# Key attention: partial sums of the probabilities on GpSimd, the rest on VectorE

## The chip, the cores and the metric

The kernel runs on one core of one Trainium2 chip. A core has TensorE (PE in the profile, its weight loads PEld), VectorE (DVE), ScalarE (ACT), GpSimd (POOL) and SyncE (SP, which issues DMAs here). Each engine takes its own instructions in order; engines wait for one another by semaphores. The metric is the device time of one execution in microseconds.

## The reference, cut to what matters

The whole reference is four layers of cross attention and feed-forward on an input x of 64 x 64 x 128. The change is in the feed-forward of the first layer, which is an attention with 16 heads of 8 channels, in which the softmax runs over the queries of each key. Its sum is taken over the 64 queries of a sequence:

```python
z = layernorm(x)
q, k, v = split_heads(z @ Wq), split_heads(z @ Wk), split_heads(z @ Wv)
scores = einsum('bkd,bqd->bkq', k, q) / sqrt(128)
attn = softmax(scores, axis=-1)
out = einsum('bkq,bkv->bqv', attn, v)
```

After it come the output projection, two normalizations and a gelu.

## The kernel before, in words

The work is cut into 32 tiles of two sequences, 128 rows each. `key_attention0_stage` (L592) treats one tile after another in a software pipeline. For each engine, `pipeline` (L58) is given a list of steps with a lag: in round t the engine issues, in the order of the list, step f for tile t - lag. With `straight=True` all rounds are written out, 32 rounds and as many more as the longest lag. Nothing is reordered at run time: an instruction whose semaphore is not there yet holds up everything behind it on its engine. `done(eng, sem, u)` waits until the semaphore's event for tile u has come, and `free(eng, sem, u, bufs)` waits for tile u - bufs, so that a buffer can be taken again.

For one tile the steps are these, with the names that the profile shows behind the stage's prefix f_:

- VectorE takes the statistics of the layer norm (`vector_stats`, L231, lag 0) and makes mean and variance of them (`vector_moments`, L241, lag 1).
- GpSimd turns the variance into 1 / sqrt(variance + eps) in two small instructions (`pool_rstd`, L247 and L250, lag 1). This is its only work in the rounds.
- VectorE applies mean and factor (`vector_apply`, L257, lag 2) and TensorE transposes the result and projects it.
- TensorE makes the scores of 16 heads in two halves (L753). VectorE takes the maximum over the 64 queries (L650) and subtracts it (L654), for each half (lag 5), and writes into `Pr`, a ring of six tiles of 128 x 16 x 64.
- ScalarE takes the exponential in place (L705), TensorE multiplies later with the probabilities that are not yet divided.
- VectorE, in `divide_v` (lag 7), sums the 64 probabilities of each head (L661), takes the reciprocal (L664) and multiplies the values by it (L668).
- TensorE multiplies values and probabilities (L767) and makes the output and the next layer's keys and values (L779 to L785); ScalarE squares and copies them (L715 to L720).

The order within a round is that of the lists. VectorE's is apply, softmax of half 0, softmax of half 1, moments, stats, divide_v (L676). GpSimd's list has the one step (L639). The next stage begins when all engines have ended this one.

Of the kernel before, what the change touches and what calls it, by code (L numbers as in the profile page):

```python
# [16 lines left out]
ALU = mybir.AluOpType  # L17
ACT = mybir.ActivationFunctionType
AX = mybir.AxisListType.X

P = 128
B, T, D = 64, 64, 128
NT = B // 2
# [34 lines left out]
def pipeline(eng, n, steps, straight=False, period=2):  # L58

    lags = [lag for lag, _ in steps]
    head = -(-(max(lags) + period) // period) * period
    if straight or head >= n:
        head = n

    def static(t):
        for lag, fn in steps:
            if 0 <= t - lag < n:
                fn(t - lag, (t - lag) % period)  # L70

    for t in range(head):
        static(t)
    if head < n:
        with eng.Fori(head // period, n // period) as i:
            for p in range(period):
                for lag, fn in steps:
                    fn(period * i + (p - lag), (p - lag) % period)
    for t in range(n, n + max(lags)):
        static(t)  # L80


def done(eng, sem, u, per=1):

    eng.wait_ge(sem, per * u + per)


def free(eng, sem, u, bufs=2, per=1):

    if isinstance(u, int) and u < bufs:  # L90
        return
    eng.wait_ge(sem, per * u + (per - per * bufs))
# [39 lines left out]
HEADS = 16  # L132
# [3 lines left out]
class Net:  # L136
# [6 lines left out]
    def w(self, name, lo=0, hi=None):  # L143
        at, n = COLS[name]
        return self.W[:, at + lo:at + (n if hi is None else hi)]


def opener(net, ctx, stage):


    nc = net.nc
    net.stale, net.current = net.current, []

    def sb(name, shape, dt=F32):
        return ctx.enter_context(nc.sbuf_tensor(f"{stage}_{name}", shape, dt))

    def ps(name, shape, dt=F32):
        return ctx.enter_context(nc.psum_tensor(f"{stage}_{name}", shape, dt))

    def sem(name):  # L160
        net.current.append(ctx.enter_context(nc.semaphore(f"{stage}_{name}")))
        return net.current[-1]

    return sb, ps, sem
# [427 lines left out]
def key_attention0_stage(net):  # L592
    nc, X, w = net.nc, net.X, net.w
    SCALE = D ** -0.5
    SG, HG, RING, DEPTH = 4, 4, 8, 6
    with ExitStack() as ctx:
        sb, ps, sem = opener(net, ctx, "f0")
# [4 lines left out]
        Pr = sb("Pr", [P, DEPTH, HEADS, T])  # L602
        mx = sb("mx", [P, 2, HEADS])
        sums = sb("sums", [P, 2, HEADS])
# [12 lines left out]
        s_spread = sem("spread")  # L617
        s_S, s_mx, s_sub, s_exp, s_sum = sem("scores"), sem("max"), sem("sub"), sem("exp"), sem("sum")
        s_rd, s_vs, s_z, s_zt, s_y = sem("rden"), sem("v_out"), sem("z"), sem("zt"), sem("y")
        s_sq, s_wz, s_wzs = sem("squares"), sem("wowff"), sem("wowff_out")  # L620
        s_cX = [sem("cX_even"), sem("cX_odd")]
        ln = LayerNorm(net, sb, sem, xn, s_xt)
        block = ctx.enter_context(nc.Block())

        @block.sync
        def _(sp):
            clear_stale(net, sp)

            def load_context(u, p):
                free(sp, s_y, u)  # L630
                sp.dma_start(cX[:, p, :], net.dram["ctxT"][u]).then_inc(s_cX[p], 16)
            pipeline(sp, NT, [(0, load_context)], straight=True)

        @block.gpsimd
        def _(pool):
            ln.setup(pool)
            nc.gpsimd.memset(V[:], 0.0).then_inc(s_zero, 1)

            pipeline(pool, NT, [(1, lambda u, p: ln.pool_rstd(pool, u, p))],  # L639
                     straight=True)  # L640

        @block.vector
        def _(dve):
            def softmax(half):
                def fn(u, p):
                    Sg = S[:, half, :, 0:256].rearrange("p r (h k) -> p r h k", k=T)
                    top = mx[:, p].rearrange("p (r u h) -> p r u h", r=2, u=2)[:, :, half]
                    out = Pr[:, u % DEPTH].rearrange("p (r u h) k -> p r u h k", r=2, u=2)[:, :, half]
                    dve.wait_ge(s_S, 2 * u + half + 1)
                    nc.vector.tensor_reduce(top, Sg, AX, ALU.max).then_inc(s_mx, 1)  # L650
                    dve.wait_ge(s_mx, 2 * u + half + 1)
                    free(dve, s_z, u, bufs=DEPTH)
                    free(dve, s_sum, u, bufs=DEPTH)
                    nc.vector.tensor_tensor(out, Sg, top.unsqueeze(3).broadcast_to([P, 2, HG, T]),  # L654
                                            ALU.subtract).then_inc(s_sub, 1)
                return fn

            def divide_v(u, p):
                done(dve, s_exp, u)
                free(dve, s_rd, u)  # L660
                nc.vector.tensor_reduce(sums[:, p, :], Pr[:, u % DEPTH], AX, ALU.add).then_inc(s_sum, 1)  # L661
                done(dve, s_sum, u)
                free(dve, s_vs, u)
                nc.vector.reciprocal(rden[:, p, :, 0], sums[:, p, :]).then_inc(s_rd, 1)  # L664
                done(dve, s_rd, u)
                free(dve, s_z, u)
                dst = V[:, p].rearrange("p g (h c) -> p g h c", c=40)[:, :, :, 0:8]
                nc.vector.tensor_tensor(dst, qkv[:, u % RING, 2].rearrange("p (g h c) -> p g h c", g=SG, h=HG),  # L668
                                        rden[:, p].rearrange("p (g h) c -> p g h c", g=SG).broadcast_to([P, SG, HG, 8]),
                                        ALU.mult).then_inc(s_vs, 1)  # L670

            dve.wait_ge(s_zero, 1)
            dve.wait_ge(s_wz, 1)
            nc.vector.tensor_copy(wow[:, D:2 * D], pA[:, 0:D]).then_inc(s_wzs, 1)
            nc.vector.tensor_copy(wow[:, 0:D], w("f0_wo")).then_inc(s_wzs, 1)
            pipeline(dve, NT, [(2, lambda u, p: ln.vector_apply(dve, u, p)), (5, softmax(0)), (5, softmax(1)),  # L676
                               (1, lambda u, p: ln.vector_moments(dve, u, p)),
                               (0, lambda u, p: ln.vector_stats(dve, u, p)), (7, divide_v)], straight=True)

        @block.scalar  # L680
# [1959 lines left out]
def feed_forward0(net):  # L2640
    key_attention0_stage(net)
# [153 lines left out]
```

## Time and profile before

| | |
|---|---|
| median of three runs | 1559.8 us (1554.31 to 1561.81) |
| the profiled execution | 1556.68 us |
| its span, first to last instruction | 1554.9 us |
| TensorE busy | 1308.1 us, 84% of the span |
| VectorE busy | 1018.9 us, 66% |
| ScalarE busy | 861.1 us, 55% |
| GpSimd busy | 599.4 us, 39% |
| mean granted clock of TensorE | 0.914 |

The shares are means over five stages with different limits. The stage of the change runs from about 243 to 422 us. Between the profiled execution's time and its span lie 1.8 us that the trace does not show.

### The profile page before, as it was taken

The page shows a single profiled execution, that of the slowest core. Times are in us where ns is not written, and L with a number is a line of the kernel's source. Part 1 is how long each engine was busy: PE and PEld are TensorE (multiplying, and loading weights), DVE is VectorE, ACT ScalarE, POOL GpSimd, SP SyncE. Part 2 cuts the span into 40 slices and gives each one's busy share as a digit, 9 for nine tenths or more (in the row PEclk, how much of TensorE's full clock was granted, in tenths as well). Part 3 has the DMA queues.
Part 4 walks back from the last instruction along what each step waited for, and adds up shares of the span by engine and source line. Part 5 has one row for each costly group of instructions (what it writes and reads, how often), then busy time and mean ns, then how long its engine had stood idle before and what let it go on. Part 6 is the DMA issues. An engine that isn't in the chain of part 4 may idle for free. (4 is left out here: it accounts for less than half of the span.)

```text
span 1554.9 us, 43292 instructions
## 1 busy us (share of the span) xinstructions
PE 1308.1 (84%) x15204; PEld 1006.5 (65%) x15204; DVE 1018.9 (66%) x3181; ACT 861.1 (55%) x2287; POOL 599.4 (39%) x1092
## 2 busy tenths in 40 slices
PE   5999997999679999768999599899549975777797
PEld 3677764555446666658999467677449964666576
DVE  4788855999698887533444477775612114888886
ACT  2666653777678697652222145455224435777686
POOL 4555521111065476460000375574530017663232
PEclk9999996999989999799999789999769995888899
DMA  3423220000100000156776311122113321111001
GB/s 116 174 104 116 109 92 5 13 17 17 38 2 1 2 22 21 37 176 189 207 206 204 93 44 53 59 88 68 62 56 115 105 72 43 35 37 31 12 14 42
DMA packets 101759, 112.52 MB, mean 72 GB/s; under 512 B 11456, under 2 KB 83136, under 8 KB 101440
## 3 DMA queue, kind: packets, MB, share of 16 engines
q1 hardware_dynamic: 73792, 83.75, 17.1%
q0 software_dynamic: 8192, 16.79, 3.8%
q10 hardware_dynamic: 19584, 9.44, 2.1%
q8 instruction: 118, 1.93, 0.5%
q14 instruction: 73, 0.60, 0.1%
HBM read 69.05 MB, written 40.89 MB: 71 GB/s over the span
## 5 line engine op out<-in xcount | busy, mean ns | idle before, releaser
L2404 ACT ACTIVATE a_silu<-a_banks 128x256 f32<-128x256 f32 x120 | 42.4, 382 | 126.9 <-DVE a_y L2279 89.7
L2567 PE MATMUL a_banks<-a_rowsT,a_w_up 128*128 128x256 f32 x480 | 111.8, 383 | 0.0
L489 ACT ACTIVATE a_PT<-a_ST 128x1024 f32<-128x1024 f32 x64 | 65.5, 1024 | 76.1 <-PE a_ST L556 76.1
L444 DVE TENSOR_REDUCE a_mx<-a_S 128x8 f32<-128x1024 f32 x64 | 78.1, 1220 | 32.2 <-PE a_S L529 32.0
L2567 PEld LDWEIGHTS a_banks<-a_rowsT,a_w_up 128*128 128x128 f32 x480 | 89.3, 193 | 10.8
L1154 ACT ACTIVATE a_h<-a_SO,a_w_down 128x256 f32<-128x256 f32 x128 | 50.2, 474 | 65.3 <-PE a_SO L1319 65.3
L2272 DVE TENSOR_TENSOR a_h<-a_silu,a_banks 128x256 f32<-128x256 f32 x120 | 47.5, 419 | 58.0 <-ACT a_silu L2404 57.9
L218 POOL MEMSET a_ln_half<- 128x1 f32 x3 | 0.3, 100 | 220.5 <-POOLq L1900 183.6
L1070 DVE COPY a_rowsT<-a_pX 128x256 f32<-128x256 f32 x32 | 13.6, 424 | 108.1 <-PE a_pX L1308 108.1
L529 PE MATMUL a_S<-a_qkM,a_qk 32*128 32x512 f32 x256 | 78.3, 689 | 6.1 <-DVE a_mx L444 6.1
L1095 ACT ACTIVATE a_xT<-a_pQ 128x128 f32<-128x128 f32 (+1 forms) x44 | 14.3, 325 | 117.3 <-PE a_pQ L1184 84.2
L923 POOL DMA_INDIRECT slots_in<-R,r_put x64 | 63.1, 985 | 36.6 <-DVE r_put L1040 19.5
L548 PE MATMUL a_ST<-a_qkM,a_qk 32*128 32x512 f32 x256 | 72.6, 643 | 1.4 <-ACT a_PT L489 1.4
L2600 POOL DMA_INDIRECT R<-slots_out,r_get x64 | 62.5, 977 | 19.5 <-issue 19.5
L2600 POOL DMA_INDIRECT Y<-slots_out,r_get x64 | 64.0, 1001 | 14.2 <-issue 13.9
L2453 PE MATMUL a_banks<-a_spread,a_blk 128*128 128x512 f32 x128 | 67.6, 610 | 0.0
L1330 PEld LDWEIGHTS a_pT<-a_w_down,a_h 128*128 128x128 f32 x512 | 62.1, 192 | 2.4 <-issue 0.8
L1330 PE MATMUL a_pT<-a_w_down,a_h 128*128 128x128 f32 x512 | 62.4, 275 | 0.6 <-DVE a_y L1079 0.6
L1319 PE MATMUL a_SO<-a_rowsT,a_w_up 128*128 128x256 f32 x256 | 62.7, 389 | 0.0
L2577 PEld LDWEIGHTS a_banks<-a_w_down,a_h 128*128 128x128 f32 x480 | 59.8, 192 | 2.8 <-issue 0.8
L2577 PE MATMUL a_banks<-a_w_down,a_h 128*128 128x128 f32 x480 | 60.1, 275 | 0.6 <-DVE a_y L2279 0.6
L480 ACT ACTIVATE a_qkM<-a_qk,W 128x256 f32<-128x256 f32 x128 | 54.2, 496 | 8.0 <-POOL a_qk L387 7.9
(423 smaller groups left out, 4105.1 us busy)
## 6 DMA issues: line engine op xcount, KB each, us to landing
slots_in<-Y SPq DMA_DIRECT2D x32, 512.0 KB, 3.3
a_w_up<-in_f_dram SPq DMA_DIRECT2D x40, 384.0 KB, 3.1
a_rows<-slots_in SPq DMA_DIRECT2D x72, 128.0 KB, 2.6
slots_out<-a_y ACTq DMA_DIRECT2D x72, 128.0 KB, 2.6
a_w_down<-in_f_dram SPq DMA_DIRECT2D x40, 192.0 KB, 2.9
keys_ahead<-a_ahead SPq DMA_DIRECT2D x8, 512.0 KB, 3.4
a_k<-keys_ahead SPq DMA_DIRECT2D x8, 512.0 KB
W<-in_wpack_dram SPq DMA_DIRECT2D x1, 3276.5 KB, 11.9
```

The source lines that it names most:

```text
L444: nc.vector.tensor_reduce(mx[:, p % 2, 2 * half:2 * half + 2], S[:, :, :].rearrange("p g (h k) -> p g h k", k=D), AX, ALU.max).then_inc(s_ ...
L480: i = nc.scalar.activation(qkM[:, p, :, j, :], qk[:, p], ACT.Copy, scale=w("mask4")[:, j:j + 1])
L489: nc.scalar.activation(PT[:, p % 2, 2 * half:2 * half + 2].rearrange("p g h k -> p g (h k)"), ST[:, :, :], ACT.Exp, scale=SCALE).then_inc( ...
L529: i = nc.tensor.matmul(S[:, b, :], qk[r, p, 0, :], qkM[r, p, 1].rearrange("p h k -> p (h k)"), start=True, stop=True)
L548: nc.tensor.matmul(ST[:, b, :], qk[r, p, 1, :], qkM[r, p, 0].rearrange("p h k -> p (h k)"), start=True, stop=False)
L923: nc.gpsimd.indirect_dma_start(xg[:, :], bass.IndirectOffsetOnAxis(ap=rt.put[:, kk, v:v + 1], axis=0), R[:, v, :], None).then_inc(s_put, 16)
L1319: i = nc.tensor.matmul(H[:, BANKS * p + b, CHUNK * c:CHUNK * (c + 1)], up[:, e % 2, lo:lo + P], rowsT[:, p, :], start=True, stop=True)
L1330: i = nc.tensor.matmul(pY[:, D * s:D * s + D], h[:, p, c, P * s:P * s + P], down[:, e % 2, D * c:D * (c + 1)], start=(c == 0), stop=(c == ...
L2453: nc.tensor.matmul(S[:, g, :], blk[:, p, g, :], spread[:, p, g].rearrange("p h t -> p (h t)"), start=False, stop=True).then_inc(s_S, 1)
L2567: i = nc.tensor.matmul(H[:, HC * p + b, CHUNK * c:CHUNK * (c + 1)], up[:, p, at:at + P], rowsT[:, p, :], start=True, stop=True)
L2577: i = nc.tensor.matmul(pE[:, D * s:D * s + D], h[:, p, c, P * s:P * s + P], down[:, p, D * c:D * (c + 1)], start=(c == 0), stop=(c == HC - 1))
L2600: net.nc.gpsimd.indirect_dma_start(t[:, u, :], None, rows, bass.IndirectOffsetOnAxis(ap=rt.get[:, k, u:u + 1], axis=0)).then_inc(rt.s_got[ ...
```

## The change

GpSimd gets a second step, `fold`, with lag 7. For each tile it adds the right 32 of the 64 probabilities of each head to the left 32 (`halves`), waits for its own result, and adds the right 16 of these to the left 16 (`quarters`). VectorE's sum in `divide_v` then runs over these 16 numbers of each head instead of over 64, and waits for `quarters` instead of for the exponential. The subtraction that writes into `Pr` again waits for `halves` in place of the sum. Both new tiles have two buffers.

```diff
--- before.py
+++ after.py
@@ -617,6 +617,8 @@
         s_spread = sem("spread")
         s_S, s_mx, s_sub, s_exp, s_sum = sem("scores"), sem("max"), sem("sub"), sem("exp"), sem("sum")
         s_rd, s_vs, s_z, s_zt, s_y = sem("rden"), sem("v_out"), sem("z"), sem("zt"), sem("y")
+        s_half, s_quarter = sem("halves"), sem("quarters")
+        halves, quarters = sb("halves", [P, 2, HEADS, T // 2]), sb("quarters", [P, 2, HEADS, T // 4])
         s_sq, s_wz, s_wzs = sem("squares"), sem("wowff"), sem("wowff_out")
         s_cX = [sem("cX_even"), sem("cX_odd")]
         ln = LayerNorm(net, sb, sem, xn, s_xt)
@@ -636,7 +638,17 @@
             ln.setup(pool)
             nc.gpsimd.memset(V[:], 0.0).then_inc(s_zero, 1)
 
-            pipeline(pool, NT, [(1, lambda u, p: ln.pool_rstd(pool, u, p))],
+            def fold(u, p):
+                done(pool, s_exp, u)
+                free(pool, s_quarter, u)
+                nc.gpsimd.tensor_tensor(halves[:, p], Pr[:, u % DEPTH, :, 0:T // 2], Pr[:, u % DEPTH, :, T // 2:],
+                                        ALU.add).then_inc(s_half, 1)
+                done(pool, s_half, u)
+                free(pool, s_sum, u)
+                nc.gpsimd.tensor_tensor(quarters[:, p], halves[:, p, :, 0:T // 4], halves[:, p, :, T // 4:],
+                                        ALU.add).then_inc(s_quarter, 1)
+
+            pipeline(pool, NT, [(1, lambda u, p: ln.pool_rstd(pool, u, p)), (7, fold)],
                      straight=True)
 
         @block.vector
@@ -650,15 +662,15 @@
                     nc.vector.tensor_reduce(top, Sg, AX, ALU.max).then_inc(s_mx, 1)
                     dve.wait_ge(s_mx, 2 * u + half + 1)
                     free(dve, s_z, u, bufs=DEPTH)
-                    free(dve, s_sum, u, bufs=DEPTH)
+                    free(dve, s_half, u, bufs=DEPTH)
                     nc.vector.tensor_tensor(out, Sg, top.unsqueeze(3).broadcast_to([P, 2, HG, T]),
                                             ALU.subtract).then_inc(s_sub, 1)
                 return fn
 
             def divide_v(u, p):
-                done(dve, s_exp, u)
+                done(dve, s_quarter, u)
                 free(dve, s_rd, u)
-                nc.vector.tensor_reduce(sums[:, p, :], Pr[:, u % DEPTH], AX, ALU.add).then_inc(s_sum, 1)
+                nc.vector.tensor_reduce(sums[:, p, :], quarters[:, p], AX, ALU.add).then_inc(s_sum, 1)
                 done(dve, s_sum, u)
                 free(dve, s_vs, u)
                 nc.vector.reciprocal(rden[:, p, :, 0], sums[:, p, :]).then_inc(s_rd, 1)
```

## Rows read from the trace of the kernel before

**Rows 1.** windows, full pipeline: busy us (instructions), granted clock, DMA share, GB/s

```profile
266.70:389.20 122.50, 112.71 (x2515) 71.45 (x2512) 119.03 (x251) 94.44 (x331) 18.45 (x50) 0.95 0.05 15
```

**Rows 2.** timeline of VectorE over one round: start us, us, engine, line, operation

```profile
291.19 0.17 DVE L241 BATCH_NORM_AGGREGATE f_ln_moments<-f_ln_stats 128x2 f32<-128x6 f32 x1
...
291.45 1.20 DVE L661 TENSOR_REDUCE f_sums<-f_Pr 128x16 f32<-128x1024 f32 x1
292.69 0.25 DVE L664 RECIPROCAL f_rden<-f_sums 128x16 f32<-128x16 f32 x1
...
293.18 0.34 DVE L257 TENSOR_SCALAR f_xn<-X,f_ln_moments,f_ln_rstd 128x128 f32<-128x128 f32 x1
...
296.09 0.17 DVE L241 BATCH_NORM_AGGREGATE f_ln_moments<-f_ln_stats 128x2 f32<-128x6 f32 x1
```

**Rows 3.** timeline of GpSimd, same round; brackets: idle us before, releaser

```profile
291.44 0.19 POOL L247 TENSOR_TENSOR f_ln_rstd<-f_ln_moments,f_ln_half 128x1 f32<-128x1 f32 x1 [4.08 <-DVE f_ln_moments L241]
...
291.70 0.55 POOL L250 TENSOR_TENSOR f_ln_rstd<-f_ln_rstd,f_ln_half 128x1 f32<-128x1 f32 x1
```

**Rows 4.** VectorE's instructions grouped by shape: count, busy us, mean ns, idle before

```profile
L2219 DVE TENSOR_REDUCE a_dense<-a_t 128x32 f32<-128x256 f32 x2 | 0.8, 420 | 0.1
```

**Rows 5.** timeline in the stage before this one, GpSimd and VectorE

```profile
141.45 0.55 POOL L250 TENSOR_TENSOR a_ln_rstd<-a_ln_rstd,a_ln_half 128x1 f32<-128x1 f32 x1
...
141.97 0.73 POOL L383 TENSOR_TENSOR a_rot<-a_rot 128x256 f32<-128x256 f32 x1
...
142.87 0.82 DVE L257 TENSOR_SCALAR a_xn<-X,a_ln_moments,a_ln_rstd 128x128 f32<-128x128 f32 x1
142.87 0.73 POOL L387 TENSOR_TENSOR a_qk<-a_rot,a_qbias 128x256 f32<-128x256 f32 x1 [0.17 <-POOL a_rot L383]
```

**Rows 6.** GpSimd's instructions grouped by shape, the whole execution

```profile
L2062 POOL TENSOR_TENSOR a_spread<-a_biased,W 128x512 f32<-128x512 f32 x32 | 33.4, 1042 | 5.5 <-PE a_banks L2453 3.4
...
L387 POOL TENSOR_TENSOR a_qk<-a_rot,a_qbias 128x256 f32<-128x256 f32 x32 | 23.6, 738 | 3.9 <-POOL a_rot L383 2.7
...
L2067 POOL TENSOR_TENSOR X<-X,W 128x128 f32<-128x128 f32 x32 | 15.5, 483 | 0.0
```

**Rows 7.** timeline where VectorE waits for GpSimd's second rstd instruction

```profile
244.13 0.55 POOL L250 TENSOR_TENSOR f_ln_rstd<-f_ln_rstd,f_ln_half 128x1 f32<-128x1 f32 x1
244.79 0.34 DVE L257 TENSOR_SCALAR f_xn<-X,f_ln_moments,f_ln_rstd 128x128 f32<-128x128 f32 x1 [0.83 <-POOL f_ln_rstd L250]
```

**Rows 8.** timeline of the stage's last rounds, VectorE and then ScalarE

```profile
389.22 0.17 DVE L241 BATCH_NORM_AGGREGATE f_ln_moments<-f_ln_stats 128x2 f32<-128x6 f32 x1
...
390.53 0.25 DVE L664 RECIPROCAL f_rden<-f_sums 128x16 f32<-128x16 f32 x1
...
406.49 0.69 DVE L654 TENSOR_TENSOR f_Pr<-f_S,f_mx 128x512 f32<-128x512 f32 x1
...
410.68 0.28 ACT L715 ACTIVATE f_junk<-f_pY 128x128 f32<-128x128 f32 x1 [1.29 <-PE f_pY L785]
...
420.79 0.28 ACT L715 ACTIVATE f_junk<-f_pY 128x128 f32<-128x128 f32 x1 [1.47 <-PE f_pY L785]
```

**Rows 9.** windows of two other stretches, columns as in the first group

```profile
1000.00:1010.00 10.00, 6.80 (x107) 5.30 (x105) 6.72 (x26) 3.24 (x7) 8.12 (x11) 1.00 0.17 50
1470.00:1480.00 10.00, 6.05 (x18) 3.39 (x17) 6.68 (x31) 5.38 (x14) 3.81 (x8) 0.50 0.02 4
```

**Rows 10.** timeline of TensorE, granted clock 0.50 until about 277 us

```profile
271.55 0.80 PE L738 MATMUL f_pA<-f_xT,W 128*128 128x128 f32 x2
...
276.77 0.80 PE L738 MATMUL f_pA<-f_xT,W 128*128 128x128 f32 x2
...
281.75 0.45 PE L779 MATMUL f_pY<-f_cX,W 128*64 128x64 f32 x8
...
283.00 0.66 PE L753 MATMUL f_S<-f_spread,f_qkv 32*64 32x256 f32 x8
```

## Prediction

> **What bounds the kernel now.** The diff touches one stage, the key attention (243 to 422 us), so I read the windows of that stage first, then one round of its pipeline instruction by instruction. From 266.7 to 389.2 us the pipeline is full: VectorE is busy 119.03 of 122.50 us, TensorE 112.71, ScalarE 94.44, GpSimd 18.45 [rows 1]. VectorE is the bound. The timeline of one round shows why: from one aggregate of layer-norm statistics to the next it takes 296.09 - 291.19 = 4.90 us, without idle time, and 1.20 us of it is the sum over the probabilities [rows 2]. GpSimd does two tiny instructions in a round and then waits 4.08 us, each time for VectorE's aggregate [rows 3]. This last column is the one to read: GpSimd is idle, but its work in a round begins only when VectorE has given it the moments.
>
> **The change, part by part.** Call round t the t-th pass over VectorE's list: apply(t-2), the two halves of softmax(t-5), moments(t-1), stats(t), divide_v(t-7). GpSimd's round t becomes rstd(t-1), then fold(t-7). Both are written straight, in order.
>
> *Removed from VectorE.* The sum goes from 1024 elements into 16 to 256 into 16. The nearest row is a reduction of 256 elements into 32, 0.42 us [rows 4]. So it saves 1.20 - 0.42 = 0.78 us a round [rows 2, 4].
>
> *Added to GpSimd.* An add of 128x512 and one of 128x256. For the second there are rows of the same size, 0.73 us (mean 738 ns) [rows 5, 6]. For the first the nearest row is L2062, 128x512 in 1.04 us, but both its operands are broadcasts; L2067 (128x128) takes 0.48 us in the mean and L387 (128x256) 0.74 [rows 6]. A straight line through these two gives 0.74 + 2 x 0.255 = 1.25 us; twice the 128x256 row gives 1.48. I take 1.28, between the line and the row with full operands doubled, nearer to the line, and keep 1.04 and 1.48 as bounds. Between the two adds lies a wait on GpSimd's own semaphore: L387, which waits in the same way for L383, shows 0.17 us of idle time [rows 5]; its lower bound I set at 0.08, the gap between the aggregate's end (291.19 + 0.17) and GpSimd's start at 291.44 [rows 2, 3].
>
> The Trainium skill (GPSIMD Engine Reference, section 3.1) speaks against such a move: it gives 4497 ns on GpSimd against 2293 ns on VectorE for an fp32 add of 2048 elements, because two inputs share one read port. By an estimate pro rata from that page the two adds would be 1.12 and 0.56 us, 0.33 less than my 2.01, and the sum below 8.6 us less. The trace agrees on the direction; its 128x256 row is dearer than pro rata, so the rows are used.
>
> *The wait that is added.* divide_v(t-7) now waits for fold(t-7). The data are old: the exponential of a tile runs right after its second subtraction, two rounds before its sum. But fold(t-7) stands behind rstd(t-1) in GpSimd's queue, and rstd(t-1) waits for moments(t-1), which VectorE issues in the same round t, two instructions ahead of divide_v(t-7). So the fold cannot begin before the moments of the same round, and VectorE stands still until it is finished. Behind the waiting sum on VectorE stand the reciprocal, the product for V, the next apply and the next softmax; TensorE and ScalarE wait for these.
>
> The chain, from the start of the aggregate (291.19 is 0):
> - first rstd instruction at +0.25, second at +0.51 [rows 2, 3]
> - next GpSimd instruction 0.52 after the second (141.45 to 141.97) [rows 5]: halves at +1.03
> - halves 1.28 and the wait 0.17: quarters at +2.48; quarters 0.73: done at +3.21
> - GpSimd's end to VectorE's start, 244.13 + 0.55 to 244.79, 0.11 [rows 7]: sum at +3.32
> - sum 0.42 and 0.04 to the next instruction (as 291.45 + 1.20 to 292.69) [rows 2]: reciprocal at +3.78.
>
> Before, the reciprocal starts at 292.69, +1.50 [rows 2]. So a round is 2.28 us longer: 7.18 in place of 4.90 us. The statistics (about 0.2 us) lie under the chain in either case.
>
> *How many rounds.* A round has this chain where it holds both a moments and a divide_v: t = 7 to 32, 26 rounds. The last of them has no statistics; its reciprocal stands at 390.53 - 389.22 = 1.31 before [rows 8], so it loses 2.47. Together 25 x 2.28 + 2.47 = 59.5 us. In rounds 33 to 38 there is no rstd, GpSimd runs ahead, and the shorter sum is pure gain. Three of these sums (tiles 26 to 28) precede the last subtraction at 406.49; after it ScalarE and TensorE set the end, draining the last outputs at 2.53 us each (410.68 to 420.79, four steps) [rows 8]. So 3 x 0.78 = 2.3 us come back. ScalarE, 3.78 us a round when full [rows 1] and less where no new tiles come in, leaves room for it. The later sums gain nothing.
>
> *Rest.* The subtraction waits for halves instead of sums of six tiles before, long done; two more semaphores are cleared and two small buffers taken: nothing, since SP and memory wait for no one there (if that cover were gone, a few tenths of a us once).
>
> Sum against the profiled execution: 1556.7 + 59.5 - 2.3 = 1613.9 us. That execution lies 3.1 us under the median of the three runs shown, 1559.8, which would give 1617.0. I say **1615**.
>
> Bounds of the costs: with 1.04 us and 0.08 us of wait a round loses 1.95, and the sum is 26 x 1.95 - 2.3 = +48, 1605; with 1.48 us and a quarters add 0.1 us dearer it loses 2.58, +65, 1622.
>
> **The rivals.**
> *The fold is hidden and the change gains.* Place: GpSimd's queue. If fold(t-7) were served before rstd(t-1), VectorE would find it done. For it: GpSimd is idle 4.08 us a round, and the fold needs about 2.2 [rows 3, 5, 6]. Price: 0.78 us less in each of 26 + 3 rounds, -23 us, 1534. It would gain less where the two engines get into each other's way: the apply at L257 takes 0.34 us alone and 0.82 us when it starts together with GpSimd's add at 142.87 [rows 2, 5], which here would take back 0.48 of the 0.78, 1548. It decides as soon as quarters end less than 0.26 us after the aggregate starts, where the sum stands now [rows 2]. Against it: GpSimd's list is in order, and the row of its idle time names the aggregate. 4 in 100.
>
> *TensorE becomes the bound at the lower clock.* The stage is at 0.95 of the full clock before [rows 1]. TensorE's 112.71 us in 25 rounds are 4.51 a round, 92% of 4.90 and 63% of 7.18. Other stretches at about that share show both levels: 6.80 of 10 us busy at a granted clock of 1.00 (2.4 GHz), 6.05 of 10 at 0.50 (1.2 GHz) [rows 9]. At the lower level one round of TensorE without the output projection is 271.55 to 276.77, 5.22 us without a gap; the projection is 283.00 - 281.75 = 1.25 at the full clock, and I bound it at 2.0 to 2.5 at half [rows 10]. That is 7.2 to 7.7 us a round against VectorE's 7.18: 0 to 0.5 us more in each of 26 rounds, up to +13, and a few us in the drain, which hangs on TensorE too. 1617 to 1632, say 1627. Against it: in the stage before, the clock rose to full in the round in which TensorE had no gap left (after 276.77 the same instructions are shorter), and a TensorE that becomes the bound has no gap. 13 in 100.
>
> *The adds are dearer than any row.* The new operands are 16 pieces of 32 and of 16 elements in a row, and the rows here have long pieces [rows 6]. Half as much again on both, 1.0 us a round, gives 1640. 5 in 100.
>
> **How the numbers follow.** The forecast with its bounds 1605 to 1622 has 78 in 100. The range reaches down to 1601, the lower bound less the scatter of the runs (7.5 us from lowest to highest, half of it), and up to 1630, which takes in most of the case of the clock. It leaves out the gain, the dearest adds and a tail. A measurement of this kernel can tell about 0.5%, 8 us, from no change. Faster by more than that: 0.04; within it: 0.01, if the fold were hidden and the gain eaten; slower: 0.95, all other cases.
>
> **What would show it.** Right: in the full rounds VectorE is idle some 2.8 us just before the sum, released by GpSimd's quarters; rounds are 7.2 us apart; halves start 0.52 us after the second rstd instruction; the sum takes 0.42 us; in the last six rounds that idle time is gone. Wrong: halves that start before the aggregate of their round, a halves add outside 1.0 to 1.5 us, TensorE at 1.2 GHz through the stage with scores waited for by VectorE's maximum, or a stage that is not 45 to 75 us longer.

## The result, and the profile after

The changed kernel takes 1614.37 us (median of three runs, 1612.24 to 1615.17) against 1559.8: 54.6 us more. The ratio is 1.033, with an interval of 1.028 to 1.038. Its profiled execution took 1615.17 us, with a span of 1613.3. One of the eight runs of the last experiment below took 3042.9 us, about twice the others, and its ratio leaves that run out.

VectorE's timeline over one full round, from aggregate to aggregate; it answers to [rows 2]:

```profile
288.19 0.17 DVE L241 BATCH_NORM_AGGREGATE f_ln_moments<-f_ln_stats 128x2 f32<-128x6 f32 x1
288.27 0.26 DVE L231 BATCH_NORM_STATS2 f_ln_stats<-X 128x6 f32<-128x128 f32 x1
291.33 0.42 DVE L673 TENSOR_REDUCE f_sums<-f_quarters 128x16 f32<-128x256 f32 x1 [2.79 <-POOL f_quarters L648]
291.78 0.25 DVE L676 RECIPROCAL f_rden<-f_sums 128x16 f32<-128x16 f32 x1
...
295.19 0.17 DVE L241 BATCH_NORM_AGGREGATE f_ln_moments<-f_ln_stats 128x2 f32<-128x6 f32 x1
```

The round is 295.19 - 288.19 = 7.00 us long. The sum is down from 1.20 to 0.42 us, but ahead of it VectorE now stands idle for 2.79 us, released by the quarters. GpSimd's timeline in the same round shows what it waits for, beside [rows 3]:

```profile
288.44 0.19 POOL L247 TENSOR_TENSOR f_ln_rstd<-f_ln_moments,f_ln_half 128x1 f32<-128x1 f32 x1 [4.14 <-DVE f_ln_moments L241]
288.71 0.55 POOL L250 TENSOR_TENSOR f_ln_rstd<-f_ln_rstd,f_ln_half 128x1 f32<-128x1 f32 x1
289.22 1.26 POOL L644 TENSOR_TENSOR f_halves<-f_Pr 128x512 f32<-128x512 f32 x1
290.56 0.74 POOL L648 TENSOR_TENSOR f_quarters<-f_halves 128x256 f32<-128x256 f32 x1
```

GpSimd still waits for the aggregate, here 4.14 us, and starts the halves 0.51 us after the second instruction of the factor. All four instructions lie between the aggregate and the sum. The waits of the stage, 267 to 445 us (us in total, times, longest), show the two engines waiting for each other by turns:

```profile
POOL f_ln_rstd L247 <- DVE f_ln_moments L241: 107.2, 26, 4.1
DVE f_sums L673 <- POOL f_quarters L648: 69.9, 25, 2.8
```

The second line is the only wait of VectorE that the profile lists in that stretch; there is none for TensorE.

GpSimd's groups by shape give the price of the two adds, beside [rows 6]:

```profile
L644 POOL TENSOR_TENSOR f_halves<-f_Pr 128x512 f32<-128x512 f32 x32 | 40.5, 1264 | 8.0 <-ACT f_Pr L717 8.0
...
L648 POOL TENSOR_TENSOR f_quarters<-f_halves 128x256 f32<-128x256 f32 x32 | 23.5, 735 | 2.5
```

VectorE's timeline in the last rounds, beside [rows 8]:

```profile
445.83 0.25 DVE L676 RECIPROCAL f_rden<-f_sums 128x16 f32<-128x16 f32 x1
446.12 0.59 DVE L680 TENSOR_TENSOR f_V<-f_qkv,f_rden 128x128 f32<-128x128 f32 x1
446.63 0.82 DVE L257 TENSOR_SCALAR f_xn<-X,f_ln_moments,f_ln_rstd 128x128 f32<-128x128 f32 x1
...
453.89 0.69 DVE L662 TENSOR_REDUCE f_mx<-f_S 128x8 f32<-128x512 f32 x1 [1.52 <-PE f_S L765]
...
461.79 0.69 DVE L666 TENSOR_TENSOR f_Pr<-f_S,f_mx 128x512 f32<-128x512 f32 x1
```

The reciprocal at 445.83 is that of the last round with a moments step. From it to the last subtraction it is 15.96 us, exactly as before (406.49 - 390.53). The product for V takes 0.59 us (0.29 before) and the apply 0.82 us (0.34 before), beside folds that GpSimd now runs one after another, and the maximum at 453.89 waits 1.52 us for TensorE. TensorE's timeline ahead of that maximum, down to the scores it waits for, shows the last matmul of the output at 1.15 us, where it takes 0.70 at the full clock:

```profile
452.08 1.15 PE L797 MATMUL f_pY<-f_wow,f_zT 128*128 128x256 f32 x2
453.16 0.66 PE L765 MATMUL f_S<-f_spread,f_qkv 32*64 32x256 f32 x8
```

Such stretches began before, as the window over 20 full rounds shows (columns as in [rows 1]); below it stands one over 19 full rounds of the kernel before:

```profile
302.19:442.23 140.04, 119.69 (x2098) 75.53 (x2097) 81.36 (x202) 84.28 (x280) 54.08 (x80) 0.72 0.04 12
```

```profile
296.10:388.90 92.80, 84.86 (x1994) 54.14 (x1994) 90.16 (x191) 73.69 (x266) 14.02 (x38) 1.00 0.06 17
```

TensorE's granted clock was 0.72 in the mean in the changed kernel's rounds, a mixture of 1.0 (2.4 GHz) and 0.5 (1.2 GHz), where it was 1.00 in the window of before; TensorE had 119.69 us of work in 140.04. Some of the rounds pass wholly at 0.50 without a gap in TensorE, but at most two in succession, and all 25 are 6.99 to 7.01 us long.

### The profile page after: what moved, and what is told of

It is laid out like the page before. It is cut to its first block and busy times, and to the rows that moved or that the text cites. A ratio compares the mean times of both kernels' runs of the same rounds, so it can differ in the third digit from the quotient of the medians.

```text
span 1613.3 us, 43418 instructions
## 1 busy us (share of the span) xinstructions
PE 1350.0 (84%) x15204; PEld 1032.1 (64%) x15204; DVE 998.1 (62%) x3181; ACT 870.3 (54%) x2287; POOL 663.2 (41%) x1156
## 5 line engine op out<-in xcount | busy, mean ns | idle before, releaser
L765 PE MATMUL f_S<-f_spread,f_qkv 32*64 32x256 f32 x512 | 56.9, 524 | 5.3 <-DVE f_Pr L666 3.8
```

The source lines that it names most:

```text
L765: i = nc.tensor.matmul(S[64 * b:64 * b + 64, half, r, 0:256], qkv[rows, u % RING, 1, T * b:T * b + T], spread[rows, p, b].rearrange("p h t ...
```

## The experiments

Theory A: the loss is a chain inside a round, moments to factor to fold to sum, because the fold stands behind the factor in GpSimd's queue. Theory B: GpSimd's adds cost VectorE time wherever they run. Theory C: TensorE at its lower clock sets the round. Each run was timed beside the kernel before on the same chip. A round is the time between two reciprocals of `divide_v` in the full part of the pipeline, and the table gives the usual one; some runs also have a few longer rounds, which the text names.

| run | median us | ratio to before (interval) | full round, us |
|---|---|---|---|
| before | 1559.8 to 1563.5 | | 4.90 |
| the change | 1614.4 | 1.033 (1.028 to 1.038) | 7.00 |
| fold ahead of the factor | 1564.2 | 1.000 (0.997 to 1.002) | 5.05 |
| fold unused | 1587.4 | 1.014 (1.010 to 1.018) | 5.75 |
| short sum, no fold | 1548.9 | 0.990 (0.987 to 0.994) | 4.35 |
| fold after apply | 1546.9 | 0.988 (0.985 to 0.992) | 4.35 |
| halves only | 1612.3 | 1.032 (1.028 to 1.035) | 6.45 or 7.4 |
| eighths too | 1624.8 | 1.040 (1.037 to 1.044) | 7.40 |
| halves only, less TensorE | 1596.7 | 1.019 (1.016 to 1.022) | 6.45 |
| halves only, after apply | 1550.1 | 0.992 (0.988 to 0.995) | 4.37 |

**Fold ahead of the factor.** Only the order of GpSimd's list is changed:

```diff
-pipeline(pool, NT, [(1, lambda u, p: ln.pool_rstd(pool, u, p)), (7, fold)],
+pipeline(pool, NT, [(7, fold), (1, lambda u, p: ln.pool_rstd(pool, u, p))],
```

> GpSimd's list is turned round: fold(t-7) ahead of rstd(t-1), all else as in the changed kernel. Theory A (the loss is the place of the fold in GpSimd's queue, behind a factor that waits for VectorE's moments of the same round): the wait of 2.8 us a round before the sum is gone, and with it the loss. VectorE's round is 4.90 - 0.78 = 4.12 us, plus 0.3 to 0.8 us where an apply or a product of V stands beside a fold (0.82 in place of 0.34 us and 0.59 in place of 0.29 us in the changed kernel's last rounds), so 4.4 to 4.9 us; 1545 to 1560 us. Theory B (it is the work itself: GpSimd's adds hold up VectorE wherever they run): the same 2.0 us of adds a round cost about the same again, 1600 us or more. Theory C (TensorE at its lower clock sets the round): the clock stays low, 1590 us or more.

It took 1564.2 us, the same as before the change. VectorE's timeline of a round:

```profile
334.06 0.17 DVE L241 BATCH_NORM_AGGREGATE f_ln_moments<-f_ln_stats 128x2 f32<-128x6 f32 x1
...
334.32 0.40 DVE L673 TENSOR_REDUCE f_sums<-f_quarters 128x16 f32<-128x256 f32 x1
...
335.25 1.30 DVE L257 TENSOR_SCALAR f_xn<-X,f_ln_moments,f_ln_rstd 128x128 f32<-128x128 f32 x1
336.47 0.68 DVE L662 TENSOR_REDUCE f_mx<-f_S 128x8 f32<-128x512 f32 x1
...
339.12 0.17 DVE L241 BATCH_NORM_AGGREGATE f_ln_moments<-f_ln_stats 128x2 f32<-128x6 f32 x1
```

The sum follows the statistics without any idle time, so the wait is gone and theory A holds for it. But the round is 5.06 us in place of 4.12 and a little: the apply at 335.25 takes 1.30 us in place of 0.34. GpSimd's timeline at that moment:

```profile
335.09 1.38 POOL L644 TENSOR_TENSOR f_halves<-f_Pr 128x512 f32<-128x512 f32 x1
336.54 0.74 POOL L648 TENSOR_TENSOR f_quarters<-f_halves 128x256 f32<-128x256 f32 x1
```

The halves started at 335.09, 0.16 us ahead of the apply, and ended at 336.47; the apply ended at 336.55. The 0.96 us that the apply loses are more than the 0.78 that the shorter sum saves. I had expected 0.3 to 0.8 us for this, and 1545 to 1560 us. Two rounds near the start, of 6.62 and 7.18 us, add 3.7 us in the profiled execution: TensorE has no gap in them, at a granted clock of 0.50 and 0.67.

The Trainium skill (SBUF — State Buffer, "Who interferes with whom") has a rule for this: VectorE and GpSimd share one pair of ports to SBUF, a VectorE instruction with two SBUF inputs or in a mode that uses both its ports (a tensor_scalar can enter it) contends with a GpSimd instruction that reads SBUF, and one with a single SBUF input outside that mode does not; in that mode the one issued first holds the pair and the other is fully blocked. The trace agrees in the main: the apply is a tensor_scalar that started after the add, and it ends 0.08 us after it. No row shows whether it was in that mode, and a plain wait does not fit two of the numbers: 0.08 us is less than the 0.34 us that the apply takes alone, and the add is longer too, 1.38 us in place of 1.26.

**Fold unused.** The fold stays where the change put it, and VectorE sums 64 probabilities as before, waiting for the exponential alone (`Pr` is taken again only after both the sum and the halves):

```diff
-done(dve, s_quarter, u)
+done(dve, s_exp, u)
...
-nc.vector.tensor_reduce(sums[:, p, :], quarters[:, p], AX, ALU.add).then_inc(s_sum, 1)
+nc.vector.tensor_reduce(sums[:, p, :], Pr[:, u % DEPTH], AX, ALU.add).then_inc(s_sum, 1)
```

> GpSimd makes halves and quarters as in the changed kernel, in the same place, but nothing reads the quarters: VectorE sums all 64 probabilities as before and waits only for the exponential. So the work of the fold is there and the wait of the sum is not. Theory A: the round is the 4.90 us of before plus what the two engines cost each other where the product for V and the apply fall beside the adds, 0.3 to 0.8 us: 1568 to 1581 us. Theory B: nearly all of the loss stays, 1600 us or more. Theory C: as A where the clock stays high in this stage, since VectorE has no gap.

It took 1587.4 us: over theory A's 1581, under theory B's 1600. VectorE's timeline, and behind it GpSimd's:

```profile
332.31 0.17 DVE L241 BATCH_NORM_AGGREGATE f_ln_moments<-f_ln_stats 128x2 f32<-128x6 f32 x1
...
334.10 0.66 DVE L681 TENSOR_TENSOR f_V<-f_qkv,f_rden 128x128 f32<-128x128 f32 x1
334.69 0.82 DVE L257 TENSOR_SCALAR f_xn<-X,f_ln_moments,f_ln_rstd 128x128 f32<-128x128 f32 x1
...
338.06 0.17 DVE L241 BATCH_NORM_AGGREGATE f_ln_moments<-f_ln_stats 128x2 f32<-128x6 f32 x1
```

```profile
333.35 1.27 POOL L644 TENSOR_TENSOR f_halves<-f_Pr 128x512 f32<-128x512 f32 x1
...
334.69 0.73 POOL L648 TENSOR_TENSOR f_quarters<-f_halves 128x256 f32<-128x256 f32 x1
```

The round is 5.75 us, 0.85 over that of before: the product for V takes 0.66 us in place of 0.29 and the apply 0.82 in place of 0.34, 0.37 + 0.48 = 0.85. Each lies beside one of the adds and ends 0.14 and 0.09 us after it. So there is something in theory B, but only for these two instructions; over 25 rounds it is 21 us. In the profiled execution, the slowest of the four at 1589.7 us, two rounds at 7.42 us, of which more below, and what lies about them add another 4 us; the stretch from the 26th reciprocal to the last subtraction is 6.4 us longer than before, with products for V of 0.85 to 1.33 us beside the adds and one wait of 1.90 us for TensorE.

**Short sum, no fold.** The kernel before with a sum over 16 of the 64 probabilities of each head (the other 48 are left out):

```diff
-nc.vector.tensor_reduce(sums[:, p, :], Pr[:, u % DEPTH], AX, ALU.add).then_inc(s_sum, 1)
+nc.vector.tensor_reduce(sums[:, p, :], Pr[:, u % DEPTH, :, 0:T // 4], AX, ALU.add).then_inc(s_sum, 1)
```

> The kernel before with a sum over the first 16 of the 64 probabilities of each head; 48 are left out, and there is no fold. This is the most that a shorter sum can give. Theory A with VectorE as the only bound: 4.12 us a round, 26 x 0.78 + 2.3 = 22.6 us less, 1537 us. Rival: TensorE, whose instructions of a round take 4.4 to 4.5 us at the full clock one after another, becomes the bound: 0.4 to 0.5 us less a round, 10 to 13 us, 1547 to 1550 us.

It took 1548.9 us. The round is 4.35 us, not 4.12. VectorE's timeline names the reason in the wait of the second maximum, and the window of all engines has TensorE busy for 121.72 of 122.00 us:

```profile
338.72 0.69 DVE L650 TENSOR_REDUCE f_mx<-f_S 128x8 f32<-128x512 f32 x1 [0.15 <-PE f_S L753]
```

```profile
267.00:389.00 122.00, 121.72 (x2741) 78.38 (x2734) 110.07 (x271) 107.58 (x360) 19.30 (x52) 0.92 0.06 16
```

TensorE is the next bound. So even a sum that costs nothing more to prepare gains 0.55 of the 0.78 us a round. One round near the start takes 6.76 us, at a granted clock of 0.72 in the mean.

**Fold after apply.** As the first run, and the fold of a tile also waits for an apply, so that the adds run beside maximum and subtraction:

```diff
 done(pool, s_exp, u)
+done(pool, ln.s_xn, min(u + 5, NT - 1))
...
-pipeline(pool, NT, [(1, lambda u, p: ln.pool_rstd(pool, u, p)), (7, fold)],
+pipeline(pool, NT, [(7, fold), (1, lambda u, p: ln.pool_rstd(pool, u, p))],
```

> As the run with the fold ahead of the factor, and the fold(t-7) also waits for apply(t-2), so that the adds run beside VectorE's maximum and subtraction, which have at most one input in SBUF besides PSUM, and end about 0.6 us before the moments. Theory A: the wait is gone and nothing is blocked; VectorE's round is 4.12 us or TensorE's 4.4 to 4.5 us: 1537 to 1550 us, the same as the short sum without a fold, and under the kernel before. Theory B: 1600 us or more. If the adds still hold up the maximum or the subtraction, they show more than 0.69 us each, and the time is above the short sum's.

It took 1546.9 us, the same as the short sum without a fold within the intervals, and beats the changed kernel by 4% and the one before by 1.2%. VectorE's timeline, and behind it GpSimd's:

```profile
330.90 0.17 DVE L241 BATCH_NORM_AGGREGATE f_ln_moments<-f_ln_stats 128x2 f32<-128x6 f32 x1
...
332.10 0.34 DVE L257 TENSOR_SCALAR f_xn<-X,f_ln_moments,f_ln_rstd 128x128 f32<-128x128 f32 x1
332.36 0.68 DVE L663 TENSOR_REDUCE f_mx<-f_S 128x8 f32<-128x512 f32 x1
333.07 0.69 DVE L667 TENSOR_TENSOR f_Pr<-f_S,f_mx 128x512 f32<-128x512 f32 x1
...
335.25 0.17 DVE L241 BATCH_NORM_AGGREGATE f_ln_moments<-f_ln_stats 128x2 f32<-128x6 f32 x1
```

```profile
332.57 1.26 POOL L645 TENSOR_TENSOR f_halves<-f_Pr 128x512 f32<-128x512 f32 x1 [0.61 <-ACT f_Pr L718]
333.92 0.74 POOL L649 TENSOR_TENSOR f_quarters<-f_halves 128x256 f32<-128x256 f32 x1
```

The same two adds of 1.26 and 0.74 us are there. The apply at 332.10 is over after its usual 0.34 us, and the maximum and the subtraction beside the adds take 0.68 and 0.69 us, as in a kernel without a fold. These have one SBUF input at most, so this side of the Trainium skill's rule agrees too. Theory B is down to the two instructions of the run before.

The profiled execution shows one thing that was not expected, in two windows:

```profile
285.00:315.00 30.00, 30.00 (x444) 18.89 (x442) 16.89 (x44) 17.75 (x58) 11.22 (x17) 0.56 0.04 11
320.00:390.00 70.00, 70.00 (x1690) 45.61 (x1688) 65.36 (x161) 65.51 (x227) 44.30 (x65) 1.00 0.07 19
```

TensorE has no gap in either. In the first its clock is 0.56 in the mean, and it holds three rounds of 7.4 us and one of 7.03; in the second the clock is 1.00 and the rounds are 4.35. These four rounds cost 12 us in this execution, the slowest of the six (1553.9 us).

**Halves only.** The changed kernel without its second add; VectorE sums 32 numbers of each head:

```diff
-done(pool, s_half, u)
-free(pool, s_sum, u)
-nc.gpsimd.tensor_tensor(quarters[:, p], halves[:, p, :, 0:T // 4], halves[:, p, :, T // 4:],
-                        ALU.add).then_inc(s_quarter, 1)
...
-nc.vector.tensor_reduce(sums[:, p, :], quarters[:, p], AX, ALU.add).then_inc(s_sum, 1)
+nc.vector.tensor_reduce(sums[:, p, :], halves[:, p], AX, ALU.add).then_inc(s_sum, 1)
```

> The changed kernel without its second add: GpSimd makes halves alone, in the same place behind the factor, and VectorE sums the 32 numbers of each head that remain. Theory A (a chain from the moments through GpSimd to the sum): 0.73 us of the second add and 0.08 us of its wait are gone, the sum of 512 elements takes 0.69 in place of 0.42 us: the full rounds are 7.00 - 0.81 + 0.27 = 6.46 us apart, and the whole is 26 x 0.54 = 14 us under the changed kernel, 38 to 44 us over the kernel before, 1598 to 1607 us. Theory B (GpSimd's busy time costs, wherever it lies): busy time falls from 2.0 to 1.26 us a round, so the loss of 55 us falls to 35 us, and the rounds come to 6.2 us.

It took 1612.3 us, not 1598 to 1607. Of the 25 distances between the first 26 reciprocals, 13 are 6.44 to 6.47 us, theory A's number, and 12 are 6.96 to 7.43. VectorE's timeline in one of the long ones:

```profile
381.93 0.17 DVE L241 BATCH_NORM_AGGREGATE f_ln_moments<-f_ln_stats 128x2 f32<-128x6 f32 x1
...
384.26 0.69 DVE L669 TENSOR_REDUCE f_sums<-f_halves 128x16 f32<-128x512 f32 x1 [1.98 <-POOL f_halves L644]
...
388.02 0.69 DVE L658 TENSOR_REDUCE f_mx<-f_S 128x8 f32<-128x512 f32 x1 [0.88 <-PE f_S L761]
...
389.36 0.17 DVE L241 BATCH_NORM_AGGREGATE f_ln_moments<-f_ln_stats 128x2 f32<-128x6 f32 x1
```

The wait for the halves is the expected 1.98 us, but the second maximum waits another 0.88 us for TensorE's scores. Two windows of all engines, TensorE first, in this round and in a stretch soon after it:

```profile
384.30:391.70 7.40, 7.40 (x107) 4.50 (x106) 4.40 (x11) 4.21 (x14) 1.97 (x3) 0.50 0.04 11
396.00:402.00 6.00, 4.70 (x113) 2.96 (x113) 3.91 (x10) 4.45 (x15) 1.97 (x3) 1.00 0.05 14
```

In the long round the clock is 0.50 and TensorE has no gap; in the other stretch it is 1.00 again and TensorE has 4.70 us of work in 6.00. So theory C, which adds nothing to the changed kernel's rounds, takes over in the stretches at 1.2 GHz, where TensorE's 7.4 us are more than the chain's 6.45.

**Eighths too.** The other way: a third add of 128x128 in the fold, and a sum over 8 numbers of each head:

```diff
+done(pool, s_quarter, u)
+free(pool, s_sum, u)
+nc.gpsimd.tensor_tensor(eighths[:, p], quarters[:, p, :, 0:T // 8], quarters[:, p, :, T // 8:],
+                        ALU.add).then_inc(s_eighth, 1)
...
-nc.vector.tensor_reduce(sums[:, p, :], quarters[:, p], AX, ALU.add).then_inc(s_sum, 1)
+nc.vector.tensor_reduce(sums[:, p, :], eighths[:, p], AX, ALU.add).then_inc(s_sum, 1)
```

> The changed kernel with a third add in GpSimd's fold, of 128x128, and a sum over the 8 numbers of each head that remain: VectorE has still less to do. Theory A: the chain is longer by the add (0.46 us) and its wait (0.08) and shorter by 0.13 us of sum, 7.41 us a round, 11 us over the changed kernel, 1620 to 1632 us. If VectorE's own work were the bound, the round would be 0.13 us shorter, 3 us under the changed kernel, 1608 to 1616 us.

It took 1624.8 us. VectorE's sum in two rounds:

```profile
382.32 0.28 DVE L678 TENSOR_REDUCE f_sums<-f_eighths 128x16 f32<-128x128 f32 x1 [3.33 <-POOL f_eighths L653]
...
389.72 0.29 DVE L678 TENSOR_REDUCE f_sums<-f_eighths 128x16 f32<-128x128 f32 x1 [3.33 <-POOL f_eighths L653]
```

The sum is down to 0.29 us, its wait up to 3.33 us, and the round is 7.40 us. Less work for VectorE and a longer time, by the 0.4 us a round that the chain gave. TensorE at the lower clock would need about the same 7.4 us, but it does not set these rounds: the one at 338.21 us is 7.40 us long at a clock of 1.00, with TensorE busy for 5.06 us of it, and VectorE's only wait in the full rounds is that for the eighths.

**Halves only, less TensorE.** The run with halves alone, without the matmuls for the next layer's keys and values; VectorE sets these to zero once, ahead of the rounds:

```diff
-for g in range(2):
-    for b in range(2):
...
-        nc.tensor.matmul(pY[q, 256 + T * g:256 + T * g + T], w("a1_wk")[:, 64 * g:64 * g + 64],
...
-        nc.tensor.matmul(pY[64 * h:64 * h + 64, 384 + 64 * b:448 + 64 * b],
...
```

> The run with halves alone, whose rounds were 6.45 us at TensorE's full clock and 7.4 us in stretches with the granted clock at 0.50, where TensorE had no gap. Here the sixteen small matmuls of a round for the next layer's keys and values (L779 and L783) are left out, 1.05 us a round at the lower clock; these keys and values are zero. If TensorE at 1.2 GHz is what makes the long rounds, its round there is 7.42 - 1.05 = 6.37 us, less than the chain's 6.45, and all full rounds are 6.45 to 6.5 us apart whatever the clock: 25 x 6.45 from the first sum's reciprocal to the 26th, 161 us in place of 170.7. If the long rounds come from GpSimd or VectorE, they stay. The whole: 1596 to 1606 us.

It took 1596.7 us, and every full round is 6.44 to 6.50 us long. The window over its middle:

```profile
300.00:430.00 130.00, 117.46 (x1830) 67.93 (x1832) 87.53 (x202) 84.49 (x283) 39.40 (x60) 0.57 0.04 12
```

The clock was lower still, 0.57 in the mean against 0.66 in the same window of the halves alone, and it does not matter. So the long rounds of the halves were TensorE's.

**Halves only, after apply.** The same wait for apply as above, with halves alone. The median of eight runs is 1550.1 us; the profile is of a ninth, of 1551.7 us.

> The fold that waits for apply, with halves alone: GpSimd's work is 1.26 us a round in place of 2.0, VectorE's 0.27 us more. If VectorE's 4.12 us and TensorE's 4.35 us are the bounds, the round is 4.39 us, VectorE's by a little, and the time is that of the fold with both adds, 1544 to 1552 us. If GpSimd's adds cost VectorE something there after all, it is shorter than that kernel by up to 5 us.

> The same kernel as the run with halves alone after apply, for a profile of its rounds: 4.39 us apart at TensorE's full clock (VectorE's 4.12 + 0.27), 7.4 us in the first rounds as long as the clock is low; the adds beside maximum and subtraction leave these at 0.69 us.

The ratio is 0.992, not to be told from that of both adds (0.988). The full rounds are 4.37 us, the three longest, near the start, 5.97 to 7.43. VectorE's timeline of a full round:

```profile
314.17 0.17 DVE L241 BATCH_NORM_AGGREGATE f_ln_moments<-f_ln_stats 128x2 f32<-128x6 f32 x1
...
314.44 0.67 DVE L670 TENSOR_REDUCE f_sums<-f_halves 128x16 f32<-128x512 f32 x1
...
318.54 0.17 DVE L241 BATCH_NORM_AGGREGATE f_ln_moments<-f_ln_stats 128x2 f32<-128x6 f32 x1
```

VectorE has no wait in it, and the 4.37 us are those of before less what the sum saves, 4.90 - (1.20 - 0.67). So the add costs VectorE nothing in that place, and half the work on GpSimd does not make the kernel faster.

## Why the prediction was right, point by point

**The wait and its place** were right, and the runs show them. The signs named in advance came: 2.79 us of idle time before the sum, halves 0.51 us after the second instruction of the factor, a sum of 0.42 us, and no idle time before five of the last six sums (0.70 us before the very last). Turning round GpSimd's list takes away the 2.8 us of idle time and the whole loss; making the chain 0.4 us longer while VectorE's work shrinks makes the round 0.4 us longer; shortening it by 0.55 makes the rounds that TensorE does not set 0.55 shorter.

**The size of the round** was 0.18 us too large. The adds were right: 1.264 and 0.735 us measured against 1.28 and 0.73, and 0.42 for the sum. By an estimate pro rata from the Trainium skill (GPSIMD Engine Reference, section 3.1) the first was 1.12, under what was measured. Two terms were mis-sized. The wait between the adds is 0.08 us (289.22 + 1.26 to 290.56), not 0.17. The trace of before had both values for that wait: from L383 to L387 it is 0.08 us in 16 of the 32 tiles and 0.16 to 0.19 in the other 16, and the forecast took one of these; what made them longer is open. And GpSimd hands over to VectorE in 0.03 us (290.56 + 0.74 to 291.33), not 0.11; why it took longer in [rows 7] no run shows. From round 7's aggregate to the 26th reciprocal the changed kernel needs 445.83 - 267.19 = 178.6 us and the one before 390.53 - 266.68 = 123.9: 54.8 us more, where 59.5 were forecast.

**The gain in the last rounds** did not come: 2.3 us forecast, none measured. The three sums are shorter by 0.78 us each, but the product for V is 0.30 us longer, the apply 0.48, and TensorE is 1.52 us late, 2.30 in all. The sum of the prediction asked only whether ScalarE leaves room for this gain; it was the folds beside VectorE's instructions and TensorE at its lower clock that took it. The rival of the clock did name the drain.

**The rest** differs by 3.6 us between the two profiled executions, 0.5 ahead of that aggregate and 3.1 behind the last subtraction. I take it for scatter, though no run shows that: the time from the next stage's start to the end was 1129 to 1133 us in the profiles of eight experiments, 1132.7 before and 1135.8 after. Together 54.8 + 0.0 + 3.6 = 58.4 us of span, where 59.5 - 2.3 = 57.2 were forecast. That 1615 is so near the median of 1614.4 is partly luck: the full rounds were forecast 4.7 us too dear, and the 2.3 us that did not come back and the 3.6 us of the rest make up for it.

**The hidden fold**, the rival on the other side, became true in the run that turns the list round, and its prices were wrong: 1534 us, or 1548 with the apply held up, against 1564, which is no gain. I had seen the apply of 0.82 us beside an add, but the add of 128x512 holds it for longer, and with all waits gone TensorE stops the gain at 4.35 us a round.

**TensorE at the lower clock** was bounded well: 7.2 to 7.7 us a round forecast, 7.42 to 7.43 measured in four kernels of the experiments. In the changed kernel it did not set the full rounds; the clock was low there in stretches only. The argument against it, that a TensorE without a gap gets its clock back, is not borne out as it stands: in the fold after apply TensorE had no gap in three rounds of 7.4 us at a granted clock of 0.50, and the clock rose only in the fourth.

**The dearer adds**, the third rival, did not come: with pieces of 32 and 16 elements in a row the adds took what the rows of long pieces gave (1.264 us against 1.25 by the line, 0.735 against 0.738).

## What to carry to other kernels

Before work goes to an idle engine, read what that engine waits for: an engine that waits 4 us a round for the very engine it is to relieve has no free time between that event and the next use of its result. Work that is ready early must stand ahead of such a wait in its queue, not behind it. And put GpSimd's reads of SBUF beside VectorE's instructions that read PSUM; the same two adds cost VectorE 0.96 us a round where the apply ran beside the first of them, and nothing beside maximum and subtraction.

## What the runs showed of the hardware

- A VectorE tensor_scalar of 0.34 us from SBUF to SBUF took 1.30 us beside a GpSimd add of 128x512 that had started 0.16 us earlier, and the add itself 1.38 in place of 1.26. A product of two SBUF tensors that started 0.75 us after such an add took 0.66 us in place of 0.29. A maximum and a subtraction that read PSUM kept their 0.68 and 0.69 us beside the same adds.
- In the halves alone TensorE's granted clock was 1.00 in a stretch with 4.70 us of work in 6.00 and 0.50 in others; its round without a gap is 4.35 us at 1.00 (short sum, fold after apply) and 7.42 at 0.50. The shorter chain bought almost nothing there: a ratio of 1.032 against 1.033.
- Between the two adds of GpSimd, with a semaphore between them, lie 0.08 us, and from GpSimd's end to VectorE's start 0.03 us.
